# In every step of the attention, VectorE takes the turned maxima and the next scan ahead of the low part and of the finished values

## The reference

```python
c_q = h @ w_down_q.T
c_kv = h @ w_down_kv.T
q = (c_q @ w_up_q.T).reshape(b, s, H, DH).transpose(0, 2, 1, 3)
k = (c_kv @ w_up_k.T).reshape(b, s, H, DH).transpose(0, 2, 1, 3)
v = (c_kv @ w_up_v.T).reshape(b, s, H, DH).transpose(0, 2, 1, 3)
q = _apply_rope_subspace(q, DR)
k = _apply_rope_subspace(k, DR)
scores = jnp.einsum('bhqd,bhkd->bhqk', q, k) * scale
attn = jax.nn.softmax(scores, axis=-1)
out = jnp.einsum('bhqk,bhkd->bhqd', attn, v)
out = out.transpose(0, 2, 1, 3).reshape(b, s, H * DH)
out = out @ w_out.T + residual
```

## Time and profile before

| | |
|---|---|
| median of 3 runs | 1506.65 us (1506.58 to 1506.79) |
| the profiled execution | 1505.08 us, span 1502.7 us |
| before the first step of the attention | 57.4 us |
| the 32 groups | 57.4 to 1316 us |
| the experts and the end | 1316 to 1502.7 us |

### The profile page before, as it was taken

The page is one execution under the profiler, slowest core; times in us unless marked ns, Lnnn a source line. Parts: engine busy times, 40 slices in busy tenths (PEclk is TensorE's granted clock), DMA queues, the critical chain, the costliest instruction groups (busy, mean ns, idle before and its releaser), DMA issues. The chain is left out here.

```text
span 1502.7 us, 45158 instructions
## 1 busy us (share of the span) xinstructions
PE 1399.5 (93%) x17865; PEld 930.2 (62%) x17865; DVE 1166.6 (78%) x2685; ACT 1066.0 (71%) x2072; POOL 1216.6 (81%) x731
## 2 busy tenths in 40 slices
PE   4899999999999999999999999999999988969995
PEld 1366665666666656666665656666666555659995
DVE  7788787777788788877788788777887888945576
ACT  2677787778877877778787777777887765724444
POOL 5588898888888988889889888899789878826275
PEclk8799999999999999999999999999999999979997
DMA  5444443423233324333333323233232242133222
GB/s 169 117 114 114 114 110 84 115 69 82 65 87 83 76 72 107 79 79 79 84 86 87 79 73 88 76 82 83 72 93 67 63 160 67 44 117 99 69 53 81
DMA packets 101489, 132.87 MB, mean 88 GB/s; under 512 B 16673, under 2 KB 51233, under 8 KB 100897
## 3 DMA queue, kind: packets, MB, share of 16 engines
q1 hardware_dynamic: 98208, 123.70, 30.8%
q0 software_dynamic: 3072, 6.30, 1.4%
HBM read 20.49 MB, written 14.94 MB: 24 GB/s over the span
## 5 line engine op out<-in xcount | busy, mean ns | idle before, releaser
L1222 ACT ACTIVATE probs<-psum 128x512 f32<-128x512 f32 x1024 | 615.2, 604 | 190.3 <-PE psum L932 189.1
L1970 POOL TENSOR_TENSOR probs_lo<-probs 128x1024 f16<-128x1024 f32 x301 | 624.8, 2086 | 117.0 <-ACT probs L1222 116.0
L1518 DVE CUSTOM_DVE_ANT_0 scan_out<-psum,ahead 128x512 f16<-128x512 f32 x512 | 349.4, 686 | 199.0 <-PE psum L827 189.7
L951 PE MATMUL psum<-cv,probs 128*128 128x66 f16 x4096 | 476.3, 193 | 12.6 <-POOL probs_lo L1970 12.1
L953 PE MATMUL psum<-cv,probs 128*128 128x64 f16 x4096 | 475.9, 193 | 0.0
L955 PE MATMUL psum<-cv,probs_lo 128*128 128x66 f16 x4096 | 474.6, 192 | 0.0
L953 PEld LDWEIGHTS psum<-cv,probs 128*128 128x128 bf16 x4096 | 380.5, 97 | 110.7 <-issue 3.0
L951 PEld LDWEIGHTS psum<-cv,probs 128*128 128x128 bf16 x4096 | 385.4, 97 | 73.6 <-POOL probs_lo L1970 13.3
L930 PE MATMUL psum<-q_both,k_twice 128*128 128x512 f16 x1024 | 388.8, 380 | 2.8 <-ACT probs L1222 2.8
L932 PE MATMUL psum<-q_max,k_ones 65*128 65x512 f16 x1024 | 391.1, 382 | 0.0
L955 PEld LDWEIGHTS psum<-cv,probs_lo 128*128 128x128 f16 x4096 | 380.0, 98 | 0.0
(11 more groups left out here) (222 smaller groups left out, 1854.8 us busy)
## 6 DMA issues: line engine op xcount, KB each, us to landing
t_swapped<-t_sin SPq DMA_DIRECT2D x248, 128.0 KB, 2.0
k_twice<-qk_hi SPq DMA_DIRECT2D x128, 128.0 KB
q_lone<-qk_hi SPq DMA_DIRECT2D x64, 128.0 KB, 2.3
q_both<-qk_hi SPq DMA_DIRECT2D x64, 128.0 KB
q_both<-qk_lo SPq DMA_DIRECT2D x64, 128.0 KB
q_max<-qk_hi SPq DMA_DIRECT2D x64, 128.0 KB, 2.3
k_ones<-qk_lo SPq DMA_DIRECT2D x64, 128.0 KB, 2.4
z_unit<-slots_in SPq DMA_DIRECT2D x31, 128.0 KB, 2.3
```

Of the source, the lines that this page charges most:

```text
L951: pe.matmul(acc, high[:, q * P:(q + 1) * P, 1], v[:, 0:VLO], start=opens, stop=False, skip_group_check=True)
L1222: act.activation(probs[s % 4][:, i, :], score_ps[tile % SCORE_BANKS], ACT.Exp, scale=SCALE).then_inc(probs_done, 1)
L1518: dve.tensor_tensor_reduce(scan_out[m % 2][:], bank[BANK_OF["base", n, m]], ahead[m % 2][:], 1.0, LOWEST, ALU.add, ALU.max, max_all[a][:, ...
L1970: pool.tensor_tensor(probs_lo[s % 4][:].rearrange("p a n -> p (a n)"), p, p.bitcast(BF16).rearrange("p (n two) -> p n two", two=2)[:, :, 1 ...
```

## The change

On VectorE, the call that does the low part of the step before and the finished values (`lagged`) moves behind `take_maxima` and `scan` of the same step. The other work of a step stays behind all of these. Nothing changes on the other engines.

```diff
             def attend(g):
                 for s in range(STEPS):
-                    lagged(g, s, g > 0)
                     if g and s == TURN_STEPS[1]:
                         take_maxima(g, 1)
                     if g < LAST:
                         if s == TURN_STEPS[0]:
                             take_maxima(g + 1, 0)
                         scan(g + 1, s)
+                    lagged(g, s, g > 0)
                     for c in range(CHUNKS):
                         if g and s == ATTN_STEPS[c]:
                             split_attention(g - 1, c)
```

## The result

| | before | changed |
|---|---|---|
| median | 1506.62 us (1506.31 to 1506.79, 4 runs) | 1563.93 us (1562.92 to 1569.55, 4 runs) |
| ratio | 1 | 1.0392, interval 1.0378 to 1.0406 |
| span of the profiled execution | 1502.7 us | 1560.7 us |

What follows compares the result with a forecast made beforehand. TensorE, busy 93%, was taken to have little slack left, with 30.7 us of waits for VectorE to gain. Terms 38 + 6 + 9 - 20 = +33 us on 1506.65 gave 1540 us; range 1500 to 1568.

Steps and rivals of the forecast that it cites:

- The turn and its price: VectorE's low part, at S+2.52 (S: step's start on TensorE), waits out GpSimd's, begun S+2.29: 2.74 us in place of 1.21.
- Term A: Steps 5 and 6: the last projection waits for the attention's low copy behind the low part; +38 us, bounds +8 to +41.
- Term B: Step 9: the base matmul waits for the late scan of step 8; +6 us, bounds 0 and +15.
- Term C: End of a group: values matmuls wait for the low parts of steps 10 and 12; +9 us, bounds 0 to +32.
- the sign given for "too low": On TensorE: waits for L1539 before L951 of more than 10 us would show the forecast too low.
- Term D: TensorE's waits for turned maxima (7.5 us), L811's for the scan (3.7), part of L827's (9) go; -20 us, bounds -14 to -31.
- That the average price holds: Rival on VectorE's low parts: they keep their average price and the gain comes through; -10 us, 1497 us, chance 0.15.
- That the waits pile up: Rival: VectorE becomes the bound, GpSimd's low parts of steps 11 to 15 come late; +74, 1581 us, chance 0.12.

Runs made afterwards that it cites:

- experiment 2: The kernel before with the change in every step but step 5: 1564.35 us, ratio 1.0408.
- new order with fills: The changed kernel with GpSimd's low part replaced by two fills with zeros that read nothing: 1490.77 us, ratio 0.9901 to the kernel before.
- old order with fills: The kernel before with GpSimd's low part replaced by two fills with zeros that read nothing: 1492.75 us, ratio 0.9912.
- experiment 3: The kernel before with the change in every step but 3 and 5: 1525.57 us, ratio 1.014.
- Experiment 9: The kernel before with only the turned maxima moved ahead of the low part, scan and finished values where they were: 1508.04 us, ratio 1.0012.

## Why the prediction was right, and where it was too low

**The turn and its price: right.** It said that the scan starts at S+1.91, the low part at S+2.52, GpSimd's at S+2.29, and that VectorE's would then take 2.74 us. Step 3 of the group shown has 1.87, 2.49, 2.29 and 2.77 us. It had the low copy of the attention at S5+5.19 and the projection of step 6 at S5+5.95; they are at 5.19 and 5.92 (the projection follows the copy by 0.05 us, where 0.07 was taken). The way there is another: the low part of step 4 doesn't start at S5+2.52, it is held up until 3.65 by the late one of step 2, and the same GpSimd instruction sets its end either way. That is why experiment 2, without the change in step 5, lost all the same. The prediction had named this ("the scan of step 4 and the rotation behind it are late in the same way") and had not drawn that step 3 was a cause of its own.

**Term A: too low, 50 us in place of 38.** Two steps of its working failed. The value of 1.3 us a group was taken below the worked-out 1.42, for groups in which GpSimd might be late; 23 groups lose 1.1 to 1.8, with a median of 1.40 and a mean of 1.38. And the start S+1.91 was worked out from the base matmul alone. The scan also needs `ahead` from ScalarE, and in six groups the table loads make that late, which costs 1.6 us more in each. 23 x 1.38 = 32 us and six groups of 3.0 = 18 us are the 50. So the upper bound given, 41 us, was not a bound.

**Term B: right.** +6.0 us in step 9, 6 forecast.

**Term C: too low, 16.6 us in place of 9, and in the main by other paths.** What the term describes, values that wait for the low parts of steps 10 and 12, is there: 0.2 us in step 13, and in step 15 eight waits of together 5.5 us, each ending 0.12 us behind L1539's end (the profile counts them under "issue"). One of them, timelines of VectorE and PEld, group 13:

```profile
625.45 2.54 DVE L1539 TENSOR_TENSOR probs_lo<-probs 128x1024 f16<-128x1024 f32 x1
...
628.10 0.10 PEld L951 LDWEIGHTS psum<-cv,probs 128*128 128x128 bf16 x1 [1.07 <-issue]
```

So a wait is rare and long, not frequent and short. The rest had no part in the term. Step 11 alone has +6.8 us, where L827 and L904 wait 6.5 us for the scan of step 10, in the first five groups. Steps 14 and 1 wait 9.6 us for GpSimd's low parts, 5.8 before. In step 15 of the three groups with the routing, L885 waits 9.3 us, 4.3 before, and as long in the new order with fills (9.5; 3.0 in the old order with fills): this part needs no turn behind a low part of GpSimd. Of the 9.7 us that the profile puts down to L951 for L1539, 8.8 are in step 5 and belong to term A. With the 5.5 us of step 15 it is 15 us, so the sign given for "too low" (more than 10 us) came. The terms are not independent either: steps 11, 14, 15, 0 and 1 have 25.6 us in experiment 3 and 18.0 in the full change.

**Term D: 16.4 us gained, 20 forecast,** if steps 4, 8, 10 and 12 are taken for it. The waits themselves fell as it said, by 7.5 us for the maxima and 3.5 for L811; of L827's for the scan, those in steps 6, 8, 12, 13 and 15 fell from 15.4 to 0.5 us, where 9 was taken, and new ones stand in steps 5, 9 and 11 (21.1 us). Experiment 9 shows that a wait removed is no gain by itself.

Sum: 50 + 6 + 16.6 - 16.4 = 56 us, and 1.9 outside these steps. The mechanism was forecast; the size was not: 57 us in place of 33. The time lies 4 us inside the range's upper end of 1568, so the range held narrowly.

**The rivals.** That the average price holds (1497 us) needed VectorE's low part to be first; it is later by 0.20 us, and L1539's mean went to 2065 ns. That the waits pile up (1581 us) had the upper ends of all terms at once: A passed its end and C stayed at half of it.

**The signs given.** L1539's mean was to be 2.2 us or more and is just under it, 2171 ns from 75 to 1285 us (2065 over all). VectorE's busy share rose by 3 points, not by 5, because the span grew too. One sign had the wrong direction: GpSimd's low part was to fall toward 1.89 us and its mean rose to 2103 ns. By the step in which it starts (groups 0 to 28), its mean fell in step 5 from 2.34 to 1.89 us and in step 7 from 2.23 to 2.02; in steps 12 and 14 it rose from 2.28 to 2.75 and from 2.36 to 2.82. The turns were not moved from one engine to the other, there are more of them: 108 of VectorE's low parts found one of GpSimd's already running, 21 before, and 41 took less than 1.25 us, 103 before.

What stays open: the share of experiment 3's end of group (11 us in step 15) that comes from each single step between 7 and 15 was not taken apart. Nor was what the order of step 3 costs by itself.

## What to carry to other kernels

- Before an instruction with two SBUF inputs is moved on VectorE, look up what GpSimd starts in the same stretch: where the move makes VectorE second, it waits out GpSimd's instruction and then takes most of its own time. Here a start 0.20 us behind GpSimd's made it 2.77 us long in place of 1.21.
- Look up every input of the instruction that is moved ahead. The scan needed `ahead` too, and where ScalarE was late with it, the low part behind it was late for nothing.
- An average duration that hides two cases is no price. Take the row of the case that the change makes.
- A wait of TensorE in the profile is an upper bound for what its removal gains: 7.5 us of waits for the maxima, removed alone, gained nothing in the time.

## What the runs showed of the hardware

- VectorE's low part (two inputs in SBUF, 128 x 1024) takes 1.21 us alone. In the changed kernel it found a GpSimd low part running 108 times, and 107 times it ended 1.08 to 1.09 us behind that one's end; the form with one 16-bit input takes 0.68 us alone and ends 0.55 to 0.57 behind. So nearly all of its time comes after the wait.
- Where VectorE waits and GpSimd has its next instruction ready, VectorE's comes in between: at 762.45 GpSimd's low part ended, VectorE's ran to 763.52, and GpSimd's next, begun at 762.40, took 2.25 us in place of 1.27. Once in the 108 it was otherwise: at 1291.62 two GpSimd instructions went first, and VectorE's took 4.83 us.
- GpSimd's fills (951 ns for 128 x 1024 of 16 bits) don't hold up VectorE's instruction with two inputs: timelines of both, where they overlap fully (the new order with fills):

```profile
706.07 0.95 POOL L1971 MEMSET probs_lo<- 128x1024 f16 x1
707.08 0.95 POOL L1973 MEMSET probs_lo<- 128x1024 f16 x1
...
706.29 1.22 DVE L1540 TENSOR_TENSOR probs_lo<-probs 128x1024 f16<-128x1024 f32 x1
```
